# Last layer's token gather: three bfloat16 products of exact parts in place of one float32 product

## The reference

```python
router_logits = silu(hidden_states @ router_w1) @ router_w2
expert_probs = softmax(router_logits.transpose(0, 2, 1), axis=-1)
expert_weights, token_indices = top_k(expert_probs, cap)          # cap = 32
expert_weights = expert_weights / (expert_weights.sum(-1, keepdims=True) + 1e-09)
expert_inputs = vmap(lambda h, i: h[i])(hidden_states, token_indices)
gate = silu(einsum('becd,edf->becf', expert_inputs, w1))
value = einsum('becd,edf->becf', expert_inputs, w2)
expert_out = einsum('becf,efd->becd', gate * value, w3)
# times the weights, then added back to the rows of the chosen tokens
```

## Time and profile before

| | |
|---|---|
| time, median of 3 runs | 517.43 us |
| time, lowest to highest | 515.69 to 517.9 us |
| profiled execution, span | 513.1 us |
| profiled execution, own time | not recorded beside its span; the median lies 4.3 us above the span |
| TensorE busy | 487.3 us (95%) |
| VectorE busy | 354.2 us (69%) |
| ScalarE busy | 288.2 us (56%) |
| GpSimd busy | 234.4 us (46%) |

### The profile page before, as it was taken

How to read it: one execution, slowest core, us unless ns; L and a number is a source line. 1 busy time by engine, 2 the same in 40 slices (tenths; PEclk the granted TensorE clock), 3 DMA queues, 4 the chain that set the end, 5 groups by cost and what they waited for, 6 DMA issues and landing times.

```text
span 513.1 us, 13570 instructions
## 1 busy us (share of the span) xinstructions
PE 487.3 (95%) x5109; PEld 378.7 (74%) x5113; DVE 354.2 (69%) x1000; ACT 288.2 (56%) x984; POOL 234.4 (46%) x331
## 2 busy tenths in 40 slices
PE   4799999998999999999999999899999999999996
PEld 3466766656668778887787777788757897799995
DVE  5888989766786678566786665757866588535553
ACT  3366566463586776666867657665664444413332
POOL 4845545035365544575444755324231980090440
PEclk9699999999999999999999999999999999999999
DMA  8900000000001100111000000022202100000001
GB/s 229 234 3 4 3 3 3 3 1 8 4 1 32 34 20 16 34 33 34 3 2 2 4 3 3 1 66 64 64 0 71 56 0 1 1 22 24 1 2 42
DMA packets 21872, 14.48 MB, mean 28 GB/s; under 512 B 5928, under 2 KB 21136, under 8 KB 21808
## 3 DMA queue, kind: packets, MB, share of 16 engines
q1 hardware_dynamic: 20704, 13.31, 9.6%
q10 hardware_dynamic: 1104, 0.30, 0.3%
HBM read 12.30 MB, written 1.05 MB: 26 GB/s over the span
## 4 chain that ended last, share of the span: by engine, by line
PE 79%; DVE 12%; ACT 3%; issue 2%; DMA 1%; POOL 1%; ACTq 0%; DVEq 0%; POOLq 0%
PE bank L1792 9%; PE bank L1721 6%; PE bank L1551 5%; PE bank L1558 5%; PE bank L1801 5%; PE bank L1538 5%; PE bank L1510 5%; PE bank L1374 5%; PE bank L1463 5%; PE bank L1521 4%; PE bank L1530 4%; PE bank L1808 3%; PE bank L1609 3%; PE bank L1359 3%; ACT work L1150 2%
## 5 line engine op out<-in xcount | busy, mean ns | idle before, releaser
L1150 ACT ACTIVATE work<-bank,negmax 128x124 f32<-128x124 f32 x256 | 90.0, 387 | 52.2 <-DVE ipa_s L775 52.0
L498 POOL TENSOR_TENSOR work<-work,rsum 128x496 f32<-128x496 f32 x64 | 64.1, 1012 | 120.2 <-DVE rsum L789 120.2
L533 POOL TENSOR_SCALAR work<-work,slot 128x128 f32<-128x128 f32 x64 | 49.7, 792 | 48.3 <-DVE slot L864 29.4
L1150 ACT ACTIVATION_READ_ACCUMULATOR work<-bank,negmax 128x1 f32 x256 | 58.9, 230 | 0.0
L1792 PE MATMUL bank<-work 128*128 128x256 f32 x224 | 53.4, 381 | 0.0
L1014 DVE SCALAR_TENSOR_TENSOR work<-work,bank 128x256 f32<-128x256 f32 x64 | 26.9, 421 | 33.0 <-ACT work L1302 32.8
L1302 ACT ACTIVATE work<-bank 128x256 f32<-128x256 f32 x64 | 24.5, 383 | 40.6 <-PE bank L1792 29.1
L481 POOL TENSOR_TENSOR work<-work 128x512 f32<-128x512 f32 (+2 forms) x48 | 39.2, 817 | 12.1 <-DVE work L745 9.6
L306 DVE TENSOR_TENSOR x_all<-bank,x_all 128x128 f32<-128x128 f32 x16 | 4.7, 292 | 57.4 <-PE bank L1721 55.4
L1792 PEld LDWEIGHTS bank<-work 128*128 128x128 f32 x224 | 40.3, 190 | 4.7 <-DVE work L1017 0.2
L773 DVE TENSOR_REDUCE negmax<-bank 128x4 f32<-128x496 f32 x64 | 42.5, 664 | 0.0
(11 more groups left out here) (197 smaller groups left out, 1101.1 us busy)
## 6 DMA issues: line engine op xcount, KB each, us to landing
work<-in_L_ffn_w_dram SPq DMA_DIRECT2D x42, 128.0 KB, 2.3
x_all<-in_x_dram SPq DMA_DIRECT2D x4, 256.0 KB, 5.8
out_dram<-x_all SPq DMA_DIRECT2D x4, 256.0 KB, 2.6
ctx_all<-in_ctx_dram SPq DMA_DIRECT2D x4, 192.0 KB, 6.0
ctx_all<-in_L_ffn_w_dram SPq DMA_DIRECT2D x6, 128.0 KB, 2.3
work<-in_L_xattn_Wq_dram SPq DMA_DIRECT2D x1, 512.0 KB, 6.5
work<-in_L_xattn_Wo_dram SPq DMA_DIRECT2D x1, 512.0 KB, 8.2
work<-in_L_ffn_We_dram SPq DMA_DIRECT2D x1, 512.0 KB, 5.7
```

The source lines that it names most:

```text
L498: pool.tensor_tensor(part, part, rsum1[:, b % 2, CH * n:CH * n + CH].unsqueeze(2).broadcast_to((128, CH, ORG)), ALU.mult).then_inc(Z.norm, 1)
L533: ins = pool.tensor_scalar(ohw_of(e)[:, k, :], count[:, :], slot[:, h, 0, k, e % E1:e % E1 + 1], slot[:, h, 1, k, e % E1:e % E1 + 1], ALU. ...
L1150: ins = act.activation(p1[:, b % 2, n, c, 0:ORG], blocks(bank[n])[:, c, 0:ORG], ACT.Exp, bias=negmax1[:, b % 2, h:h + 1], accum_out=sums1[ ...
```

## The change

The float32 tokens are split into three bfloat16 parts: the token rounded to bfloat16, the rest rounded to bfloat16, and what then remains. `gather(b)` becomes three bfloat16 products that accumulate in the same bank, with the one-hot matrix in bfloat16. The split is done by GpSimd in four groups of four batch entries, `parts(0)` to `parts(3)`, of four operations each on 128 x 512, and each operation waits for the one before. GpSimd does `parts(0)` after its round 12, `parts(1)` after its round 13, `parts(2)` before `slot_rows(0)` and `parts(3)` before `slot_rows(1)`. The parts of the second half use the same memory as those of the first, so `parts(2)` and `parts(3)` wait until gather 7 is done. Each gather waits for its group.

```diff
--- before.py
+++ after.py
@@ -203,13 +203,15 @@
         count = work.take([128, 128])
         xT4_early = work.take([128, 4, 128])
         hT4 = work.take([128, 2, 4, 128])
-        oh = work.take([128, 2, E1, CAP])
+        oh = work.take([128, 2, E1, CAP], BF16)
         xn_0 = work.take([128, HB, D])
         xgT_0 = work.take([D, HB, E1, CAP])
+        xn_parts = work.take([128, HB, 3, D], BF16)
 
         words = D * 2 * F1 // 128 + F1
         work.again(attn0_end, ffn0_end)
         ew_early = [work.take([128, words]) for e in range(6)]
+        xn_rest = work.take([128, 4, D])
         work.again(ffn0_end, folds_end)
         ew_first = [work.take([128, words]) for e in range(4)]
         xn_1 = work.take([128, HB, D])
@@ -255,7 +257,7 @@
         Z = named(sem, "z", "xn xb tr xT q q_sb k0 k1 k0_sb k1_sb ki v v_sb vi0 vi1 score ipa_max maxed ipa_exp ipa_step ipa_p "
                             "exp rsum norm turned p_sb p_odd o o_sb proj x_new stats")
 
-        R = named(sem, "r", "wide count tok picks xn tr xT hid th h logit max ex step topx top turned slot")
+        R = named(sem, "r", "parts wide count tok picks xn tr xT hid th h logit max ex step topx top turned slot")
         G = named(sem, "g", "told oh got xg")
         X1 = named(sem, "x", "gv tanh a h eo eo_sb ohw")
         Y = named(sem, "y", "part sum x_new stored")
@@ -526,6 +528,20 @@
                 pool.tensor_scalar(rw2_wide[:, :].rearrange("p (b n) -> p b n", b=8)[:, :, 0:E1],
                                    rw2[:, :].unsqueeze(1).broadcast_to((D, 8, E1)), 0.5, None, ALU.mult).then_inc(R.wide, 1)
 
+            def parts(g):
+
+                wide, to = xn_half[g // 2][:, 4 * (g % 2):4 * (g % 2) + 4, :], xn_parts[:, 4 * (g % 2):4 * (g % 2) + 4, :, :]
+                pool.wait_ge(R.xn, 4 * g + 4)
+                if g >= 2:
+                    pool.wait_ge(G.got, HB)
+                pool.tensor_copy(to[:, :, 0, :], wide).then_inc(R.parts, 1)
+                pool.wait_ge(R.parts, 4 * g + 1)
+                pool.tensor_tensor(xn_rest[:, :, :], wide, to[:, :, 0, :], ALU.subtract).then_inc(R.parts, 1)
+                pool.wait_ge(R.parts, 4 * g + 2)
+                pool.tensor_copy(to[:, :, 1, :], xn_rest[:, :, :]).then_inc(R.parts, 1)
+                pool.wait_ge(R.parts, 4 * g + 3)
+                pool.tensor_tensor(to[:, :, 2, :], xn_rest[:, :, :], to[:, :, 1, :], ALU.subtract).then_inc(R.parts, 1)
+
             def slot_rows(e):
 
                 h = e // E1
@@ -545,6 +561,8 @@
                     tables()
                 if b == 9:
                     rstds(0, HB)
+                if b in (12, 13):
+                    parts(b - 12)
                 if b == 13:
                     rstds(HB, 12)
                 if b == 15:
@@ -554,6 +572,8 @@
             for e in range(2 * E1):
                 if e == 0:
                     pool.wait_ge(Z.proj, B)
+                if e in (0, 1):
+                    parts(2 + e)
                 if e % E1 == 0:
                     pool.wait_ge(R.slot, e // E1 + 1)
                 if e >= E1 + 8:
@@ -1606,8 +1626,11 @@
                 pe.wait_ge(G.oh, b + 1)
                 if b >= HB:
                     after(pe, G.xg, b - 1)
-                pe.matmul(bank[got_in(b)][:, :], xn_half[b // HB][:, b % HB, :], oh[:, b % 2, :, :].rearrange("p e s -> p (e s)"),
-                          start=True, stop=True).then_inc(G.got, 1)
+                pe.wait_ge(R.parts, 4 * (b // 4) + 4)
+                for n in range(3):
+                    mm = pe.matmul(bank[got_in(b)][:, :], xn_parts[:, b % HB, n, :],
+                                   oh[:, b % 2, :, :].rearrange("p e s -> p (e s)"), start=(n == 0), stop=(n == 2))
+                mm.then_inc(G.got, 1)
 
             def round1(b):
                 f, t, g, j = b + 1, b - 1, b + 4, head_of(b)
```

## The result

| | before | changed |
|---|---|---|
| time, median of 6 runs | 516.57 us | 513.53 us |
| lowest to highest | 515.69 to 517.9 | 511.86 to 513.81 |
| profiled execution, own time | not recorded | 513.47 us |
| profiled execution, span | 513.1 us | 511.8 us |

The ratio is 0.9936, with a 95% interval of 0.9917 to 0.9954: 3.3 us less (2.4 to 4.3). The prediction was 516.0 us from a median of 517.43, so 1.47 us less.

What follows compares the result with a forecast made beforehand. TensorE, busy 95% of 513.1 us, was taken as the bound. Gains of 2.55 us less 0.75, 0.17 and 0.16 gave 1.47 us, so 517.43 became 516.0 us, range 514.3 to 517.8.

Steps and rivals of the forecast that it cites:

- The gathers in the expert steps: Gathers 8 to 15, expert steps 11 to 14: nothing new binds, each gains 0.215 us, 1.72 us in all.
- Which of the first eight gathers give something: Last two attention rounds: gathers 3, 5 and 6 gain fully, 7 gains 0.08 us, 0, 1, 2 and 4 nothing.
- What they give: Gathers 0 to 7: 0.25 us for each of three gathers plus 0.08 for gather 7, 0.83 us gained.
- the exposed load: First weight load of a gather after a wait: 0.105 us exposed, a third of it, 0.035, saved by bfloat16.
- The price of the split on GpSimd: Each group of four operations takes 3.8 us (3.3 to 4.6); groups 0 and 1 free, slot rows end at 427.1.
- What the longer GpSimd work does to VectorE: VectorE operations wait for the GpSimd operation under way: losses of 0.75, 0.17 and 0.16 us.
- The 0.75: `topx` at 424.70, expert steps: waits for a slot row under way, loss 0.75 us (0 to 1.2), all on the path.
- The two smaller terms: Normalizing entry 15 waits 0.17 us (0 to 0.6) for group 2's first copy; L835 at 413.60 waits 0.16 (0 to 0.55).
- The level: Times lie 4.3 us above the profiled span (517.43 against 513.1), an offset carried into the forecast time.
- the first: Rival at `topx`: slot rows don't block it or GpSimd finishes earlier; gain 2.2 us, 515.2 us, chance 0.20.

Runs made afterwards that it cites:

- late_only: Kernel before with only gathers 8 to 15 changed and only groups 2 and 3 of the split: time ratio 0.9967, stretch 84.08 us against 85.7.
- split_only: Kernel before plus all four split groups on GpSimd, which nobody reads; all gathers stay float32: time ratio 1.0004, stretch 85.80 us against 85.7.
- shift_c: Changed kernel with six small GpSimd memsets after the first slot row, to shift the slot rows against `topx`: one execution, 513.7 us; stretch 82.97 us.

## Why the prediction was wrong

- *The gathers in the expert steps*, 1.72 us: right. late_only, which bears also the 0.1 that the cast and `topx` lose, gives 1.61; the chain shows 0.65 us against 0.86.
- *Which of the first eight gathers give something*: right. Gathers 0, 1, 2 and 4 gave nothing, gather 7 little; the waits are the ones named.
- *What they give*, 0.83 us: too low, 1.01 measured. A gather after a wait went from 1.05 to 0.75, 0.30 less instead of 0.25: almost all of the exposed load went, not a third of it.
- *The price of the split on GpSimd*, 3.8 us a group: 3.75 measured, right in sum because a subtraction of 1.16 us instead of 1.27 and the uncounted time between operations cancel. That the first two groups are free and the slot rows of the first half end near 427: right (427.8).
- *What the longer GpSimd work does to VectorE*, 1.08 us: **the step that failed.** "So a DVE operation of this kind waits for the GpSimd operation under way. With slot rows running until 427.1, `topx` at 424.70 meets one." The rows that it rested on, `topx` and L835 in rounds 13 and 14, were collisions with `norm`, a GpSimd operation with two tensors. Slot rows have one, and in all eleven profiles in which `topx` met one it took 0.69 to 0.71 us. The 0.75 was 0.1 (split_only). The two smaller terms were too large as well: L835 took 0.30 us in the first profile of the changed kernel and 0.38 in the second, so 0.01 to 0.09 of wait where 0.16 had been counted, and `normalize` of entry 15 met the last 0.14 us of the first cast and took 0.34 as before (0.17 counted). In the rows before, one fact pointed away from the step: L835 at 413.60 took 0.29 us beside slot rows, and the one stretched there was the slot row, to 867 ns. I read that as luck of phase. It was in part: the slot row started in the same hundredth of a microsecond as L835, and in later runs L835, further into a slot row, waited up to 0.11 us. But never for the rest of the slot row, which is what the step charged.
- *The rule of the Trainium skill* ("SBUF — State Buffer", section "Who interferes with whom") says that a VectorE instruction with two SBUF inputs and a GpSimd instruction that reads SBUF exclude each other, and that the one that starts first holds the ports for all its length. With `norm` the runs agree: `topx` started 0.11 us into one and took 1.45 us, so it was held until some 0.15 us before `norm`'s recorded end. The cast that the subtraction held for 0.88 us has only one input and isn't the case that the sentence is about. With slot rows they don't agree: in shift_c a slot row is 0.56 us under way, it reads SBUF, and `topx` runs at once. The measurement decides.
- *The level*: the 4.3 us of offset was mostly scatter of one execution, and the median of the three runs shown, 517.43, was 0.9 us above that of six.

Of the rivals, the first (no collision, 2.2 us gained) is what happened, with 0.4 us more: 0.18 from the exposed loads and the rest from the two small waits that it still counted, less the 0.1 at the cast and `topx`. The changed kernel's median lies 0.8 us below the range, and the drift of the kernel before's median, 0.9 us, would cover that; but the forecast gain of 1.47 lies outside the interval of the measured one too (3.3, 2.4 to 4.3). Of the 3.3 the stretch explains 2.6 to 2.7. The rest is no more than the interval allows, and no profile shows a gain outside the stretch.

What is shown of who gives way: `topx` met `norm` in round 14 and a slot row in expert step 9 at the same moment, about 0.1 us after the GpSimd operation's start, with the cast under way at that start. GpSimd's timeline of the kernel before at `topx` of round 14:

```profile
365.37 1.01 POOL L498 TENSOR_TENSOR work<-work,rsum 128x496 f32<-128x496 f32 x1
```

There `norm` kept its 1.01 us and `topx` took 1.45. With slot rows, in nine profiles at 0.08 to 0.13 us after the start, `topx` kept its 0.7 and the slot row was stretched to about 1.3. Two profiles have `topx` further in, at 0.56 and 0.72 us; none has it between 0.13 and 0.56, so for those phases nothing is shown.

The length of the GpSimd operation is not what decides. Slot rows have 128 columns and subtractions 512, but the kernel before has two-tensor operations of 128 columns as well (VectorE's and GpSimd's timelines):

```profile
304.38 0.61 DVE L621 TENSOR_SCALAR work<-x_all,mv,rstd 128x128 f32<-128x128 f32 x1
...
304.45 0.46 POOL L483 TENSOR_TENSOR x_all<-x_all,work 128x128 f32<-128x128 f32 x1
```

The GpSimd sum is shorter than a slot row, and yet this normalization took 0.61 us instead of 0.34, as it did in all 28 such meetings in the fourteen profiles (0.60 to 0.62), and the sum kept its 0.46. At 413.60 an operation of the same form and size, L835, started together with a slot row and kept its 0.29 us. Whether it is the number of tensors or the kind of the operation stays open: no run changes one of these alone.

## What to carry to other kernels

Before a collision between two engines is priced, look in the trace for the same pair of operations side by side, and see which of the two is stretched. Here the price was taken from another kind of GpSimd operation, and the only row with a slot row pointed the other way. A product in place of another gains only at the instructions behind which nothing waits for another engine; walking through the gathers one by one found that to 0.2 us. When a change is worth half a per cent, compare a stretch between two instructions that both kernels have, since it repeated to 0.1 us where spans of single executions scattered by more than one.

## What the runs showed of the hardware

- A VectorE cast of 128x32 waited 0.88 us for a GpSimd subtraction of 128x512 that had begun 0.13 us before it; the same cast beside one-tensor GpSimd operations of 128x128 took 0.18 to 0.33 us.
- About 0.1 us after the start of a GpSimd operation, a two-tensor VectorE operation (0.69 us alone) took 1.45 us beside a two-tensor multiply, and 0.69 to 0.71 beside a one-tensor operation of 0.79 us, which was itself stretched to 1.29 to 1.34. Beside a two-tensor GpSimd sum of 128x128 (0.46 us) a one-tensor VectorE operation took 0.61 instead of 0.34 us.
- Without a wait a float32 product of 512 columns took 0.86 us and a bfloat16 one 0.215, so one float32 product took as long as four bfloat16 ones.
- In a gather whose first weight load had waited, the first bfloat16 matmul of 512 columns is 11 ns longer than the others, the first float32 one 105 ns.
